# Attention's loop over pairs of heads: written out, or run as a loop of the engines

## The reference

```python
x = x + layernorm(attention(layernorm(x)))      # 16 heads of 64, rotary positions, causal
x = x + layernorm(ffn(layernorm(x)))            # width 2752, weights as NF4 codes and scales

# attention, for each head
logits = where(causal, q @ k.T, -1e9) / sqrt(64)
out = softmax(logits) @ v                       # then out @ Wo
```

## Time and profile before

| | us |
|---|---|
| three runs, median (lowest to highest) | 3080.8 (3079.91 to 3082.7) |
| the profiled execution, its own time | 3079.91 |
| its span, first to last instruction | 3078.1 |
| attention, first item to last product on PE | about 594 to 1283 |
| the last stage's matmuls | about 1623 to 3058 |

### The profile page before, as it was taken

One profiled execution on the slowest core, in us unless ns is written; L12 is line 12 of the kernel. 1 busy time (PEld: TensorE's weight loads), 2 busy tenths in 40 slices (PEclk: granted clock), 3 DMA queues, 4 the chain that ended last, 5 costly groups with the idle time before them and its releaser, 6 DMA issues. The chain is left out here.

```text
span 3078.1 us, 55127 instructions
## 1 busy us (share of the span) xinstructions
PE 2738.7 (89%) x19792; PEld 1476.4 (48%) x19792; DVE 2106.7 (68%) x3522; ACT 1830.1 (59%) x2483; POOL 601.1 (20%) x399
## 2 busy tenths in 40 slices
PE   4998999789999999588808999999999999999996
PEld 2443444267777777444403444444444444444442
DVE  6544555577777777345567877877777777777867
ACT  2113434268888988712267677766767667676642
POOL 0000000067778878500120000000000000000002
PEclk9998999789999999899959999999999999999998
DMA  4312222322222221112221111111111111111124
GB/s 164 119 51 89 82 75 68 89 77 77 77 76 62 73 75 49 59 62 75 74 64 55 49 50 48 48 55 46 52 49 49 50 49 48 55 50 45 53 69 164
DMA packets 84361, 209.43 MB, mean 68 GB/s; under 512 B 13840, under 2 KB 14224, under 8 KB 83856
## 3 DMA queue, kind: packets, MB, share of 16 engines
q1 hardware_dynamic: 84112, 206.17, 21.5%
HBM read 172.49 MB, written 33.62 MB: 67 GB/s over the span
## 5 line engine op out<-in xcount | busy, mean ns | idle before, releaser
L1334 PE MATMUL gp<-region,wgu 128*128 128x512 f16 x4224 | 930.3, 383 | 90.0 <-DVE wgu L1492 90.0
L1371 ACT ACTIVATE line<-code,offsets 128x512 f32<-128x512 f32 x1056 | 697.1, 713 | 111.2 <-DVE below L1470 45.5
L1334 PEld LDWEIGHTS gp<-region,wgu 128*128 128x128 f16 x4224 | 415.7, 99 | 600.9 <-issue 109.9
L732 POOL TENSOR_TENSOR pt_pair<-probs,pt_pair 128x1024 f16<-128x1024 f32 (+1 forms) x256 | 524.2, 2072 | 167.0 <-ACT probs L900 162.7
L1347 PE MATMUL yp<-wd,inter 128*128 128x512 f16 x2112 | 464.8, 381 | 24.8 <-DVE wd L1492 17.7
L940 DVE TENSOR_REDUCE mx<-sx 128x1 f32<-128x512 f32 (+3 forms) x640 | 360.6, 604 | 144.4 <-PE sx L833 115.5
L305 POOL TENSOR_TENSOR st<-st,eps 128x1 f32<-128x1 f32 x64 | 22.3, 348 | 1883.0 <-DVE st L1018 1639.2
L895 ACT ACTIVATE pt_pair<-st,coef 128x1024 f16<-128x1024 f32 (+1 forms) x320 | 318.2, 994 | 70.3 <-PE st L814 55.8
L550 PE MATMUL pq<-region,wt_pair 128*128 128x512 f16 x1536 | 334.2, 381 | 15.3 <-DVE wt_pair L601 15.3
L1347 PEld LDWEIGHTS yp<-wd,inter 128*128 128x128 f16 x2112 | 206.2, 98 | 279.8 <-issue 25.5
L900 ACT ACTIVATE probs<-st,coef 128x1024 f32<-128x1024 f32 (+1 forms) x320 | 317.8, 993 | 6.9 <-POOL pt_pair L732 6.4
(11 more groups left out here) (116 smaller groups left out, 3442.2 us busy)
## 6 DMA issues: line engine op xcount, KB each, us to landing
qk_pairs<-r_pair SPq DMA_DIRECT2D x128, 128.0 KB, 2.1
k<-qk_pairs SPq DMA_DIRECT2D x48, 256.0 KB, 5.3
cst<-in_gate_codes SPq DMA_DIRECT2D x44, 256.0 KB, 2.7
sst<-in_gate_scales SPq DMA_DIRECT2D x88, 128.0 KB, 3.0
cst<-in_up_codes SPq DMA_DIRECT2D x44, 256.0 KB, 2.7
sst<-in_up_scales SPq DMA_DIRECT2D x88, 128.0 KB, 3.0
cst<-in_down_codes SPq DMA_DIRECT2D x44, 256.0 KB, 2.8
sst<-in_down_scales SPq DMA_DIRECT2D x88, 128.0 KB, 3.1
```

The source lines that it names most:

```text
L732: eng.tensor_tensor(pt_pair[:, n0(u, g) % PT_RING, 1, 0:w], probs[:, n0(u, g) % P_RING, 0:w], pt_pair[:, n0(u, g) % PT_RING, 0, 0:w], ALU. ...
L1334: mm = pe.matmul(gp[:, e % 2, m, :], wgu[:, par, m, a, col0:col0 + P], xnT[:, b, k, tok], start=(k == 0 and a == b), stop=(k == KT - 1 and ...
L1371: a.activation(line[:, k % 4, :], code7[:, :], ACT.Identity, scale=slope, bias=offsets[:, k:k + 1]).then_inc(s_L.sem, 1)
```

## The change

In `slots` the first seven pairs become a loop of the engines, with `t` in a register; the eighth body stays written out behind it. The order of the slots is the same.

```diff
             for y in range(last_lag):
                 slot(look(0, y, False))
-            for t in range(HEADS // 2):
+            with eng.Fori(0, HEADS // 2 - 1) as t:
                 for y in range(last_lag, last_lag + PAIR):
-                    slot(look(t, y, t == HEADS // 2 - 1))
+                    slot(look(t, y, False))
+            for y in range(last_lag, last_lag + PAIR):
+                slot(look(HEADS // 2 - 1, y, True))
```

## The result

| | before, us | after, us |
|---|---|---|
| median of four runs (lowest to highest) | 3080.36 (3077.96 to 3082.7) | 3112.96 (3112.42 to 3114.22) |
| span of the profiled execution | 3078.1 | 3112.5 |
| mean granted clock | 0.960 | 0.955 |
| last product of attention on PE starts at | 1283.2 | 1314.2 |

The kernel with the loop is slower: ratio 1.0106, 95% interval 1.0094 to 1.0117, 32.6 us between the medians. The forecast was 3127 us with a range of 3096 to 3180. Nearly all of the 32.6 us is in attention: its last product is 31.0 us later. The two profiled executions differ by 34.4 us. The other 3 us lie in the last stage, from its first matmul to the end of the span (1458.1 us for 1455.0); its code is the same, and executions of one kernel differ by as much (3077.96 to 3082.7 before).

What follows compares the result with a forecast made beforehand. PE was taken to bound attention. Back-edge stops 21, low clock 8 and addresses 17 us summed to 46 on 3079.9, giving 3126; the median being 0.9 higher, 3127 us was forecast, range 3096 to 3180.

Steps and rivals of the forecast that it cites:

- (a): Attention loop's six taken back edges on PE: 21 us of stops, plus 8 us from the low clock afterwards.
- (c): Register addresses of V in PE's products: 0.3 us late in each m = 7 slot, 17 us, bounds 0 and 25.
- What bounds the kernel: In attention PE is busy 74.1 of 80 us, so a microsecond lost on PE is one of the stage.
- (a) The stop: PE idle about 3.5 us at each of six back edges (branch 3.56 us, 0.3 covered): 21 us, bounds 15 and 26.
- (a) The clock: Near 1.2 GHz after four or five of PE's six stops in attention: 8 us, bounds 0 and 10.
- (b) The targets: Semaphore targets from registers in attention's slots: taken as 0, with 0 to 14 us possible on PE.
- the bound 0: Lower bound for the V addresses' cost in attention: nothing if slack takes it, beside 17 us expected.
- Every address anew: Rival: each of a head's 72 pieces recomputes its addresses, 84 us in place of 17, 3194 us; chance 0.13, part included.
- Short back edges: Rival: PE's attention branches take 0.215 us or are hidden, 3081 to 3098 us; chance 0.12.
- The 108 ns: Skill's compare-and-branch time: by it alone six back edges cost 0.65 us, some 29 us less than the sum.
- Faster: Rival: looped attention code avoids fetch holes in PE's issue, 3076 us with short branches; chance 0.02.

Runs made afterwards that it cites:

- pe_loop_only: Against the kernel before: only PE runs the attention loop, DVE, ACT and POOL stay written out; 3113.85 us, ratio 1.0104.
- regs_true: Against the kernel before: seven pairs written out, targets and addresses from a hand-set register, no back edge taken; 3079.38 us, ratio 0.9999.
- pe_written_out: Against the kernel before: PE stays written out, DVE, ACT and POOL run the attention loop; 3078.85 us, ratio 0.9994.
- short_after: The changed kernel with two of three products of probabilities and V left out, 1626 PE instructions a body; 3054.2 us.
- short_before: The kernel before, written out, with two of three products of probabilities and V left out; 3056.33 us.
- two_pairs: Against the kernel before: loop body of two pairs, last two pairs written out, two back edges taken; 3091.7 us, ratio 1.0034.

## Why the prediction was right, and where not

The sign, the place and the mechanism were as forecast; the size was 13 us too high (46 us forecast, 32.6 measured, in the range). That the forecast came as near as it did rests on (a) alone; (c), more than a third of the sum, was not there.

- **What bounds the kernel.** Right: PE's lost time in attention was the stage's (31.6 us), with no other engine's loop adding to it (pe_loop_only 1.0104, the full change 1.0106).
- **(a) The stop.** Right in the sum: 3.5 us each was forecast and 3.59 to 3.86 came, 22.4 us for 21. This nearness is in part luck, as two of its parts were off and cancelled. The branch takes 4.4 to 4.8 us, not 3.56; and 1.0 us is covered, not 0.3, as the sequencer arrives at the branch while scores and an item are still in the queue. I had counted the last product alone. Nor were 384 and 2304 the whole of the two older bodies: with register operations, waits and the branch they have 396 and 2394 instructions, which changes nothing in the reading.
- **(a) The clock.** Right in size: 8 us for four or five edges was forecast; all six had a low clock, two for 6.8 us, and some 9 us are left for it by the estimate above.
- **(b) The targets.** Right at 0: regs_true has them all, and a stage 0.5 us longer.
- **(c) The addresses.** The counts were exact: 32 operations a head, 224 and 224 in all. Their price was the failed term: 17 us forecast, 0 measured. The start of the matmuls of one slot of m = 7 in the changed kernel shows both sides:

```profile
768.22 0.20 PE L862 MATMUL ob<-region,pt_pair 128*128 x1
768.35 0.20 PE L864 MATMUL ob<-region,pt_pair 128*128 x1
768.39 0.20 PE L866 MATMUL ob<-region,pt_pair 128*128 x1
...
768.92 0.20 PE L864 MATMUL ob<-region,pt_pair 128*128 x1
```

Where an address is new, the next matmul can come 0.13 us later in place of 0.03, so this slot's products take 1.11 us in place of 0.74, within the 1.00 to 1.14 of the sum (whose upper end had 12 ns a matmul from no row), and are late by 0.37, a little more than the 0.3 I took. But the other three slots of m = 7 lose nothing (0.74, 0.74 and 0.64 us, as before), though they have new addresses too: 14 slots are late and not 56, 5 to 6 us in all. And these don't lengthen a head, which takes 40.7 us as before. The record shows where they went: PE's wait for DVE's maxima, 28.1 us before, is 21.1 in regs_true, which has PE's registers and no edge, 22.4 in pe_loop_only, and still 27.1 in pe_written_out, where the other engines alone have registers. The error was to take a delay of the sequencer for a delay of the stage, and to do so for all slots of m = 7; the bound 0 ("if slack takes it") stood beside it and was the one that came.
- **The rivals.** Every address anew: refuted by the count. Short back edges: right as a mechanism, for another body; with 1626 instructions they are 0.215 us. The 108 ns of the Trainium skill, Advanced Engine Details and Errata, Control Flow Timing, were met by neither (0.215 us when the target is at hand, 4.6 us when not). Faster: no; short_after against short_before is 0.07% the quicker, less than can be told apart.

Where the expected gain of a shorter program could have come from was not seen: the kernel before has no hole in PE's issue, and six copies fewer saved nothing.

## What to carry to other kernels

Before turning written-out code into an engine's loop, count the instructions of PE in the body, weight loads and register operations included: with up to 1626 the back edge took 0.2 us here, from 2170 on its branch took 3.3 to 5.1 us, of which 0.7 to 1.1 us were covered by queued work, plus a clock at half for 3.4 us or more behind each stop of 3.6 us. If the body must be long, put more work into a turn (5.5 us an edge with twice the body, 5.3 with the single one), or leave PE written out and let the others loop. Delays of issue in an engine that waits for another anyway are not to be added up slot by slot: take them off that wait first.

## What the runs showed of the hardware that was not expected

The length of PE's taken branch has a step and little behind it: 0.215 us for bodies of 396 and 1626 instructions, 3.3 to 3.8 for 2170, 3.4 to 4.3 for the 2394 of the last stage, 4.4 to 5.1 for 2746 (pe_loop_only included), 5.0 to 5.1 for twice the pair. DVE's gap behind a taken branch goes from 0.3 us at 261 instructions to 3.3 at 518. A hint shortens PE's branch to 3.0 us in the median, wherever it stands, and a second stop of about 1 us follows in nine cases of twelve, while on DVE in the last stage it took the gap from 3.1 to 0.6 us. Stops of PE in attention of 3.6 us and more were always followed by the 1.2 GHz level (14 of 14 in the changed kernel, pe_loop_only and two_pairs), stops of 2.8 to 3.2 us in two cases of six, stops of 1.7 to 2.7 us in three of twelve. The length of the stop alone doesn't decide: the two of the middle group were its shortest.
